# Windowed attention on one core: scores wrapped into two 128-column blocks, masked by one addition, and the split of x spread over DMA, ScalarE and GpSimd

## What is computed

```
x = attn_layer(shift_tokens(x), ...) + x      # 16 heads of 64, window 32
x = ffn_layer(shift_tokens(x), ...) + x       # layer norm, gated gelu, 341 wide

shift_tokens: features 64..127 of token t are those of token t-1 (0 at the start)
sim[i, j] = q_i . k_j * 8, kept where j <= i and j >= i - 32 (else -max), within the
            window's own 32 tokens and the 32 before
out_i = sum_j softmax_j(sim)[i, j] * v_j
```

## Time and profile before

| | |
|---|---|
| median of 3 runs | 4308.0 us (4307.14 to 4308.48) |
| profiled execution | 4310.28 us, span 4308.2 us |
| granted TensorE clock, mean | 0.956 |
| busy PE, DVE, ACT, POOL | 85%, 84%, 71%, 63% of the span |
| instructions | 109724 |

### The profile page before, as it was taken

One profiled execution on the slowest core, in us unless ns is written; L12 is line 12 of the kernel. 1 busy time (PEld: TensorE's weight loads), 2 busy tenths in 40 slices (PEclk: granted clock), 3 DMA queues, 4 the chain that ended last, 5 costly groups with the idle time before them and its releaser, 6 DMA issues. The chain is left out here.

```text
span 4308.2 us, 109724 instructions
## 1 busy us (share of the span) xinstructions
PE 3648.7 (85%) x31072; PEld 2319.1 (54%) x31072; DVE 3618.5 (84%) x12131; ACT 3063.5 (71%) x8807; POOL 2732.3 (63%) x4419
## 2 busy tenths in 40 slices
PE   5887688898888888888988888888888888898884
PEld 2444355555555555555555555555555555555552
DVE  7999688889888888888888888888887888888873
ACT  3443477777777777777787777777776777877774
POOL 0000577777777777677776776777776767777771
PEclk8999799999999999999999999999999999999997
DMA  1000322222222222222222222222222222222221
GB/s 45 6 7 12 106 92 90 85 90 96 90 88 90 82 95 93 87 93 84 84 101 91 93 87 80 88 95 88 99 84 79 94 95 89 94 85 89 86 78 61
DMA packets 225228, 352.55 MB, mean 82 GB/s; under 512 B 41535, under 2 KB 68349, under 8 KB 224381
## 3 DMA queue, kind: packets, MB, share of 16 engines
q1 hardware_dynamic: 224604, 345.22, 23.4%
HBM read 125.41 MB, written 5.77 MB: 30 GB/s over the span
## 5 line engine op out<-in xcount | busy, mean ns | idle before, releaser
L964 POOL TENSOR_SCALAR pr<-pr,rden 128x128 f32<-128x128 f32 (+1 forms) x3072 | 1134.4, 388 | 931.7 <-DVE rden L1219 930.6
L852 ACT ACTIVATE pr<-sm,nb,rq 128x128 f32<-128x128 f32 (+1 forms) x3072 | 1515.9, 498 | 44.7 <-DVE nb L1246 39.4
L971 POOL TENSOR_TENSOR rot<-ab,swp 128x512 f32<-128x512 f32 x768 | 984.4, 1282 | 509.7 <-DMA swp<-ab 508.5
L1194 DVE TENSOR_TENSOR ab<-bank,ltab 128x512 f32<-128x512 f32 x1536 | 985.4, 683 | 281.3 <-PE bank L292 260.8
L1240 DVE CUSTOM_DVE_ANT_0 sm<-bank,mask 128x128 f32<-128x128 f32 (+1 forms) x3072 | 841.3, 330 | 55.9 <-issue 52.2
L840 ACT ACTIVATE sq<-bank 128x512 f32<-128x512 f32 x768 | 451.6, 588 | 256.7 <-DVE ab L1194 255.0
L852 ACT ACTIVATION_READ_ACCUMULATOR pr<-sm,nb,rq 128x1 f32 x3072 | 587.8, 191 | 0.0
L634 PE MATMUL bank<-ident,pr 128*128 128x128 f32 x1536 | 407.1, 291 | 210.1 <-DVE pt L1226 208.3
L1226 DVE COPY pt<-bank 128x512 f32<-128x512 f32 x768 | 531.5, 692 | 10.2
L625 PEld LDWEIGHTS bank<-rot 64*64 64x64 f32 x12288 | 291.9, 133 | 452.8 <-issue 452.4
L977 POOL TENSOR_TENSOR rot<-rot,rkb 128x512 f32<-128x512 f32 x384 | 497.7, 1296 | 44.2 <-DMA rkb<-k_scratch 44.2
(11 more groups left out here) (156 smaller groups left out, 6503.7 us busy)
## 6 DMA issues: line engine op xcount, KB each, us to landing
swp<-ab SPq DMA_DIRECT2D x1536, 128.0 KB, 2.0
rkb<-k_scratch SPq DMA_DIRECT2D x768, 128.0 KB, 2.9
raw<-Wqkv SPq DMA_DIRECT2D x48, 128.0 KB, 2.2
gg<-xT SPq DMA_DIRECT2D x48, 128.0 KB, 2.3
gg<-xT SPq DMA_DIRECT2D x48, 127.5 KB, 2.4
raw<-Wqkv SPq DMA_DIRECT2D x12, 256.0 KB, 2.7
wo<-Wo SPq DMA_DIRECT2D x6, 512.0 KB, 4.2
k_scratch<-rsum SPq DMA_DIRECT2D x192, 8.0 KB
```

Source lines behind the costliest of these rows:

```text
L852: ins = act.activation(pr[:, s % 4, i, cs], sm[:, s % 2, i, cs], ACT.Exp, bias=nb[:, s, t, i:i + 1], scale=head_scale(rq, p, b)[:, t, i:i ...
L964: ins = pool.tensor_scalar(pr[:, e % 4, i, cs], pr[:, e % 4, i, cs], rden[:, e, t, i:i + 1], 1.0, ALU.mult, ALU.mult)
L971: pool.tensor_tensor(rot[:, PAIRS * (j % 2) + j // 2, :], ab[:, j % 2, 0, :], swp[:, j % 2, :], ALU.add).then_inc(qk_rot, 1)
L1194: ins = dve.tensor_tensor(seqs(ab[:, j % 2, i, :]), seqs(use_bank("qk", j)[:, :]), ltab[:, 2 * (j % 2) + i:2 * (j % 2) + i + 1, :] .to_bro ...
```

## The change

- **Scores** use 2 x 128 columns a head. The keys before the second tile no longer have 32 columns of their own: for its first 64 queries they are written over the last 32 columns of their block, which these queries never need (`wrapped` in `constants`). `SCORE_TILES` gets a fifth entry: the third piece is divided into 64 and 32 columns.
- **Mask and maxima**: banks 0 and 1 become one PSUM tensor `pair`, so one addition masks both heads and both tiles (128 x 2 x 256, the mask broadcast over heads) into `sm`; VectorE waits for it (`sc_mask`), and one reduction takes the four maxima into `mx`, in PSUM as before.
- **Probabilities**: the block order in `pt` is turned round, with 32 more columns at the end for the corner. Since the own block of the second tile now holds the wrapped keys in the columns of its first 32 queries, VectorE waits for its copy (`p_copy`) and clears 32x64 elements of `pt`; only then is `p_Tsb` raised.
- **Normalisation** on GpSimd is one multiplication over 128 x 512 with `rden` broadcast, in place of four with a scalar.
- **The split of the next x** leaves VectorE. SP brings the shifted x into a new tile `xs2` by two transfers in step 8, ScalarE rounds it to `xh` in step 11 (`split_high_x`), and GpSimd subtracts to get `xl` in step 14 (`split_low_x`).

```diff
-SCORE_TILES = [(0, 0, 0), (1, 32, 32), (2, P, P - WINDOW), (3, P + 64, P + 32)]
+SCORE_TILES = [(0, 0, 0, 96), (1, 32, 32, 96), (2, P, P, 64), (2, 2 * P - WINDOW, P - WINDOW, WINDOW), (3, P + WINDOW, P + WINDOW, 96)]
...
+                def shift_next(x):
+                    done = held(sp_e, n.n[1] + 2) if cur is not None else None
+                    src = seqs(xT[:, bass.ds(x * GT, GT)])
+                    if done is not None:
+                        sp_e.wait_ge(x_split, done)
+                    sp_e.dma_start(seqs(xs2[:, :])[0:64], src[0:64]).then_inc(xs2_in, 16)
+                    sp_e.dma_start(seqs(xs2[:, :])[64:128, :, 1:SEQ], src[64:128, :, 0:SEQ - 1]).then_inc(xs2_in, 16)
...
+                    if s == 8 and gs[2] is not None:
+                        shift_next(gs[2])
...
-                            cs = slice(0, P) if t == 0 else slice(P, UW)
+                            cs = slice(t * P, t * P + P)
                             ins = act.activation(pr[:, s % 4, i, cs], sm[:, s % 2, i, cs], ACT.Exp,
...
+                def split_high_x(buf):
+                    landed = held(act, n.z[32] + 64 if cur is not None else n.z[32] + 32)
+                    settle(act)
+                    act.wait_ge(xs2_in, landed)
+                    act.activation(xh[:, buf, :, :], seqs(xs2[:, :]), ACT.Copy).then_inc(x_hi, 1)
...
-                    for i in range(2):
-                        for t in range(2):
-                            cs = slice(0, P) if t == 0 else slice(P, UW)
-                            ins = pool.tensor_scalar(pr[:, e % 4, i, cs], pr[:, e % 4, i, cs],
-                                                     rden[:, e, t, i:i + 1], 1.0, ALU.mult, ALU.mult)
+                    dst = pr[:, e % 4, :, 0:2 * P].rearrange("p i (t c) -> p i t c", t=2)
+                    ins = pool.tensor_tensor(dst, dst, rden[:, e, :, :].rearrange("p t i -> p i t").unsqueeze(3)
+                                             .to_broadcast([P, 2, 2, P]), ALU.mult)
...
+                def split_low_x(buf):
+                    made = held(pool, n1 + 3 if cur is not None else n1 + 2)
+                    settle(pool)
+                    pool.wait_ge(x_hi, made)
+                    pool.tensor_tensor(xl[:, buf, :, :], seqs(xs2[:, :]), xh[:, buf, :, :].bitcast(F32), ALU.subtract)\
+                        .then_inc(x_split, 1)
...
-                    dve.transpose(pt[96:128, e % 4, :, 0, P:P + WINDOW], pr[0:32, e % 4, :, P:P + WINDOW])
-                    dve.tensor_copy(pt[:, e % 4, :, :, 0:P],
-                                    bank[2][:, :].rearrange("p (i t c) -> p i t c", i=2, t=2)).then_inc(p_Tsb, 1)
+                    dve.transpose(pt[96:128, e % 4, :, 2 * P:UW], pr[0:32, e % 4, :, 2 * P - WINDOW:2 * P])
+                    dve.tensor_copy(pt[:, e % 4, :, 0:2 * P],
+                                    bank[2][:, :].rearrange("p (i c) -> p i c", i=2)).then_inc(p_copy, 1)
+                    dve.wait_ge(p_copy, n16 + (16 * q + e + 1))
+                    dve.memset(pt[96:128, e % 4, :, 0:WINDOW], 0.0).then_inc(p_Tsb, 1)
...
-                    for i in range(2):
-                        for t in range(2):
-                            cs = slice(0, P) if t == 0 else slice(P, UW)
-                            ins = dve.tensor_tensor_reduce(sm[:, s % 2, i, cs], bank[i][:, cs], mask[:, cs],
-                                                           1.0, -3e38, ALU.add, ALU.max, mx[:, t, i:i + 1])
-                    ins.then_inc(sc_max, 1)
+                    dst = sm[:, s % 2, :, 0:2 * P]
+                    dve.tensor_tensor(dst, pair[:, :, 0:2 * P], mask[:, :].unsqueeze(1).to_broadcast([P, 2, 2 * P]),
+                                      ALU.add).then_inc(sc_mask, 1)
+                    dve.wait_ge(sc_mask, n16 + (s + 1))
+                    dve.tensor_reduce(mx, dst.rearrange("p i (t c) -> p i t c", t=2), AX_X, ALU.max)\
+                        .then_inc(sc_max, 1)
...
-                    if gs[2] is not None and s == 11:
-                        if cur is not None:
-                            dve.wait_ge(v_proj, n8 + 8)
-                        split_high_x(gs[2], par)
-                    if gs[2] is not None and s in (13, 14):
-                        split_low_x(gs[2], par, n1 + 3 if cur is not None else n1 + 2, s - 13)
```

48 lines of the change are left out of this document (28 added, 20 removed).

## The result

The changed kernel takes 4353.2 us (median of 4 runs, 4348.14 to 4355.57), the kernel before 4308.2 in the same comparison: a ratio of 1.010, 95% interval 1.0084 to 1.0116. It is 45 us slower, where 107 were forecast: the direction is right, and the size is under half of the forecast. The profiled execution took 4348.14 us, span 4346.3.

What follows compares the result with a forecast made beforehand. The prediction took TensorE, VectorE and ScalarE to bound stretches A, B and C of one 75.0 us item; +1.46, +0.57 and +0.2 made 2.23 us, times 48 = 107 us, so about 4415 us, range 4262 to 4475.

Steps and rivals of the forecast that it cites:

- B: Stretch from nb(9) to nb(13), 16.8 us, said to be bound by VectorE; forecast to grow by 0.57 us an item.
- C: Stretch from nb(13) to nb(15), 11.8 us, said to be bound by ScalarE; forecast to grow by 0.2 us an item.
- A: Stretch from nb(15) to nb(9), 46.4 us, said to be bound by TensorE; forecast to grow by 1.46 us an item.
- Maxima: VectorE's addition and reduction up to nb: 1.46 us in place of 1.20, +0.26 us a step.
- Copy and clearing: VectorE's copy of the probabilities plus the 32x64 memset: 0.83 us in place of 0.61, +0.22 us a step.
- Splits leave VectorE: Work taken off VectorE: 1.35 us in step 12 and both halves of `xl`, in all 4.35 us an item.
- Scores on TensorE: Ten score matmuls for eight on TensorE: +0.10 us a step, bounds nothing to 0.14.
- ScalarE copy, GpSimd, SP: ScalarE's new copy of 0.60 us, GpSimd's normalisation and new `xl`, SP's two transfers: all forecast as hidden.
- (1): Rival: VectorE bounds the stretch nb(13) to nb(15) too, so the kernel gets faster, 4272 us; chance 0.18.
- (2): Rival: the fused maxima's accumulators are as dear as they look, -0.28 us a step with the memset, 4189 us; chance 0.06.
- (3): Rival: VectorE's reduction is held up beside GpSimd, +1.6 us in each step, some 5250 us; chance 0.02.
- (4): Rival: ScalarE bounds the stretch nb(9) to nb(13) through its new copy, +0.6 us on the sum, 4444 us; chance 0.09.

Runs made afterwards that it cites:

- attn_only: The changed kernel with the split of x back on VectorE as before: 4506.9 us, ratio 1.0452 to the kernel before.
- split_only: The kernel before with only the split of the next x moved off VectorE, and tiles packed to make room: 4231.9 us, ratio 0.9821.
- the early kernels: ScalarE's square put ahead of gelu in step 13: ratio 1.0044 in the kernel before, 0.9863 in the changed one, 0.9780 in split_only.
- after_hole: The changed kernel without the clearing; TensorE writes around the corner with two more matmuls a step: 4588.2 us, ratio 1.0644 to the kernel before.
- before_ten: The kernel before with one score piece divided, ten matmuls for eight, and nothing else: 4319.6 us, ratio 1.0005.
- after_fused: The changed kernel with the fused add-and-maximum back, four of 128 columns: 4240.9 us, ratio 0.9837 to the kernel before.
- after_noclear: The changed kernel without the wait for the copy and the clearing, so part of the computation is left out: 4242.4 us, ratio 0.9840 to the kernel before.

## Why the prediction was wrong, point by point

- **What bounds the kernel.** The three regimes hold in part. B is VectorE's while its steps are long: it takes over the growth of a step in full (attn_only: 2.70 us in four steps that grew by 0.55 each in plain form, and by more around the casts). With short steps GpSimd's queue holds step 12 (split_only). C is ScalarE's, by split_only and the early kernels. A is not TensorE's throughout: 0.7 us a step more on TensorE shows at once (after_hole), the small piece of before_ten does not, and step 7 follows VectorE's step (3.53 to 4.09 us).
- **Maxima.** Forecast 1.46 us from the addition to nb; 1.44 in the row. The reduction took 695 ns, where 0.69 us was taken from the prologue. The Trainium skill's rule of fewest operations ("VectorE: DVE Perf Modes", "Rules for kernel authors") would have made the wide form the faster one; after_fused, with four fused instructions and four reads, is 0.32 us a step faster, so here the measurement decides against it.
- **Copy and clearing.** Forecast +0.22, measured +0.29 in the row and 0.31 by after_noclear; the memset was put at 0.10 (112 ns), but the handovers at its two ends came to 0.10 instead of 0.04. A plain step grew by 0.56, not 0.48, within its bounds of 0.35 to 0.58. (The lower bound does not follow from its parts, which come to 0.18 + 0.12 = 0.30.)
- **Splits leave VectorE: this step failed.** It gave 1.35 us in B and nothing else, read in an item in which the casts ran undisturbed. Taking the split from the new attention is worth 3.54 us in the mean item (attn_only to after): 3.00 in B and 0.75 in A, less 0.21 in C. The 3.00 are casts of 1.96 us beside GpSimd, and 1.01 of waiting for TensorE in step 13, which the prediction had at nothing. The attention half alone was forecast at 1.46 + 1.92 + 0.2 = 3.58 us and measures 4.16. The sum of both errors, -2.19 and +0.58, is -1.61: the difference between 2.23 and 0.62. The trace of before had the long casts; the earlier trace rows is such a slow output, and the prediction used it as a tail of 0.75 us and not as a part of the mean.
- **A wait that the sum left out.** Sorted by stretch, half of the error is in A, and there in step 8: 1.06 us less, while the other nine steps grew by 1.71. TensorE's wait for the shifted x (80.2 us, now 59.1) and the low clock behind it in 10 items, now 2, stand in no term of the prediction. Both halves of the change shorten the step: 5.33 us before, 4.90 in attn_only, 4.95 in split_only, 4.27 after.
- **Scores on TensorE.** 0.10 us a step, 1.0 an item, 48 us in all, was mis-sized: before_ten gives +0.05% and A +0.08 us. That attn_only's A grew by 1.40, near the 1.46 forecast, is a right number for a wrong reason, and so is the 1.34 of the quiet item (step 0 took 0.61 of it where 0.2 was forecast). VectorE's longer step did it: with the clearing moved and the maxima fused, A is 47.93 us with the same ten matmuls, below the 48.42 of before. VectorE's waits in A of over 0.15 us, which the prediction took for cover, went from 7.19 to 2.94 us in the mean item.
- **ScalarE copy, GpSimd, SP.** Costed at nothing, and hidden. ScalarE's new copy takes 624 ns, B's steps around it are as short as the arithmetic of VectorE says, and the new transfers land in 2.4 us at step 8.
- **Stretch C.** Forecast +0.2; the quiet item has +0.17, the mean +0.28. The square is followed at once by the waiting projection, and the transposes' wait is gone, as described.
- **Rivals.** (1) falls by split_only: C stays at 12.04. (2) falls by after_fused. (3) falls by the row of 695 ns. (4) falls by B's 17.33 in the quiet item: 16.80 + 0.53, with no 0.6 on top. None of the four was the case that came. It was one that the prediction didn't have: the item read isn't the mean item, and the two halves of the change aren't additive.
- **What would show it.** VectorE's share was to be 86% and is 85%; the score groups were to be near 0.6 us, and before_ten shows that this doesn't reach the time. The test "TensorE's busy time unchanged" didn't tell anything: it grew by 42 us, and ten matmuls cost nothing all the same.

Step 8 is also why the slower half of the items lost nothing in steps 1 to 9 (75% quantile 43.75 to 43.36 us) while the quiet ones lost 0.7. Without step 8 that quantile goes from 37.32 to 38.67 us and the median from 36.57 to 37.76.

What stays open: which part of the change takes the low clock out of step 8. Of 46 items 10 have it before, 12 in attn_only, 2 in split_only and after, but also only 5 in before_ten and 7 in after_fused.

## What to carry to other kernels

Before one iteration is cut out of a trace to price a change, look where it stands among all iterations, and price the mean: here the quiet item gave +2.04 us and the mean +0.62. What a piece of work costs on a busy engine depends on what else was put there, and what its removal gives depends on which wait comes up in its place, so measure the halves of a change apart and together. An operation in a step that is repeated 768 times and passed along a chain between two engines costs its handovers too: 32x64 elements cleared in 0.11 us made 112 us, and on an engine with time to spare the same clearing was nearly free.

## What the runs showed of the hardware

- A plain product between transposes is dear: in after_hole the start-to-start time of the 128x32 product with 96 columns is 0.28 us, and 0.65 us for each group of three, while two whole transposes take some 0.3. In the scores, products of 96 columns follow one another at 0.56 us for eight.
- Dividing one product of 96 columns into 64 and 32 was free in time, though TensorE's busy sum grew by 30 us: its busy share doesn't tell whether a small addition is on the path.
- GpSimd's multiplication with a broadcast second operand took 1040 ns for 128x512, that with two full operands 1282.
- Casts of VectorE (64x512) take 0.42 to 0.65 us beside GpSimd's operations with a scalar and, when they start under one with two full operands, end 0.28 us after its end: 1.52 us before, 0.45 to 1.57 in attn_only, by how much of GpSimd's operation was left.
- `xl` with two SBUF operands behaves alike. Its mean of 2285 ns before is made of 23 items at 3.12 us beside three GpSimd operations, 12 at 2.28 beside two, 13 at 0.67 to 1.78 beside one or none; in attn_only, where GpSimd is idle beside it in most items, the same line takes a third:

```profile
L1176 DVE TENSOR_TENSOR xl<-xT,xh 64x512 fp32r<-64x512 f32 x48 | 39.0, 813 | 0.0
```
